# Another order of operand splits, gating steps and row tiles around the seven block products of a residual LoRA chain

## The reference

```python
x = x + x @ w_eff.T                      # layer 0: quantized weight plus a LoRA delta
x = x + (x @ W1.T + 2 * lora_1(x))       # layer 1: top-2 gates of 8 experts, rank 16 each
x = x + (x @ W2.T + b + 2 * lora_2(x))   # layer 2: one adapter per sequence, rank 16
x = x + x @ weight3[adapter].T           # layer 3: one full 1024x1024 matrix per sequence
```

## Time and profile before

| | |
|---|---|
| median of 3 runs | 658.16 us |
| the profiled execution: its time | 658.05 us |
| its span, first to last instruction | 656.2 us |
| TensorE busy | 644.5 us (98%) |
| VectorE busy | 499.8 us (76%) |
| ScalarE busy | 364.1 us (55%) |
| GpSimd busy | 89.0 us (14%) |
| DMA | 102 GB/s over the span |

### The profile page before, as it was taken

How to read it: one execution, slowest core, us unless ns; L and a number is a source line. 1 busy time by engine, 2 the same in 40 slices (tenths; PEclk the granted TensorE clock), 3 DMA queues, 4 the chain that set the end, 5 groups by cost and what they waited for, 6 DMA issues and landing times.

```text
span 656.2 us, 10322 instructions
## 1 busy us (share of the span) xinstructions
PE 644.5 (98%) x3992; PEld 591.0 (90%) x3992; DVE 499.8 (76%) x645; ACT 364.1 (55%) x549; POOL 89.0 (14%) x120
## 2 busy tenths in 40 slices
PE   8999999999999999899999999999999999999997
PEld 8899989999999999898889899889989889989886
DVE  6899899879970649858876967887886888686753
ACT  6673674961911445637664735664745665564553
POOL 2210225005010010001130001221001122000010
PEclk9999999999999999999999999999999999999999
DMA  9663112121021002132773122673213575002472
GB/s 295 190 200 91 33 35 62 33 62 35 1 64 64 1 1 89 33 97 72 231 237 98 52 75 61 197 255 124 65 33 97 162 258 182 1 1 65 127 229 94
DMA packets 46020, 67.32 MB, mean 103 GB/s; under 512 B 3604, under 2 KB 32020, under 8 KB 45972
## 3 DMA queue, kind: packets, MB, share of 16 engines
q1 hardware_dynamic: 40900, 58.28, 28.6%
q10 hardware_dynamic: 5072, 8.39, 3.5%
HBM read 58.27 MB, written 8.39 MB: 102 GB/s over the span
## 4 chain that ended last, share of the span: by engine, by line
PE 85%; DVE 13%; issue 1%; ACT 1%; DMA 1%; DVEq 0%; ACTq 0%
PE ps L1260 26%; PE ps L1262 26%; PE ps L1261 26%; DVE e_both L897 4%; PE ps L1403 3%; DVE x_both L897 2%; DVE tmp L1187 1%; PE ps L1271 1%; PE ps L1432 1%; PE ps L1405 1%; DMA xraw<-lora_b_t 1%; ACT e_both L683 1%; DVE bc_hi L897 1%; DVE e_mid_w L1160 0%; DVE e_mid_w L1123 0%
## 5 line engine op out<-in xcount | busy, mean ns | idle before, releaser
L1260 PE MATMUL ps<-e_both,ring_hi 128*128 128x384 f32 (+3 forms) x384 | 133.6, 348 | 0.0
L1262 PE MATMUL ps<-e_both,ring_lo 128*128 128x384 f32 (+3 forms) x384 | 133.5, 348 | 0.0
L1261 PE MATMUL ps<-x_both,e_both 128*128 128x256 f32 x448 | 125.6, 280 | 0.0
L897 DVE TENSOR_TENSOR e_both<-raw,e_both 128x512 fp32r<-128x512 f32 x128 | 90.3, 725 | 34.1 <-ACT e_both L771 33.4
L771 ACT ACTIVATE e_both<-raw 128x512 fp32r<-128x512 f32 x128 | 78.9, 628 | 67.0 <-PE ps L1262 66.7
L1260 PE MATMUL ps<-e_both,e_mid 128*128 128x512 f32 (+2 forms) x288 | 110.8, 385 | 0.0
L1262 PE MATMUL ps<-e_both,e_mid 128*128 128x512 f32 (+2 forms) x288 | 110.7, 384 | 0.0
L1261 PE MATMUL ps<-e_both,e_mid 128*128 128x512 f32 (+2 forms) x288 | 110.6, 384 | 0.0
L587 POOL TENSOR_TENSOR raw<-raw,ident 128x128 f32<-128x128 f32 x64 | 42.3, 662 | 360.7 <-DMA raw<-w_t 360.7
L1261 PEld LDWEIGHTS ps<-x_both,e_both 128*128 128x128 f32 x448 | 84.6, 189 | 0.0
L1262 PEld LDWEIGHTS ps<-e_both,ring_lo 128*128 128x128 f32 x384 | 72.3, 188 | 5.7
(11 more groups left out here) (175 smaller groups left out, 1271.0 us busy)
## 6 DMA issues: line engine op xcount, KB each, us to landing
raw<-w_t SPq DMA_DIRECT2D x64, 512.0 KB, 4.4
w_w<-x_t SPq DMA_DIRECT2D x16, 512.0 KB, 3.9
w_w<-w SPq DMA_DIRECT2D x15, 512.0 KB, 4.2
y<-tmp ACTq DMA_DIRECT2D x30, 256.0 KB, 3.5
e_both_w<-w_t SPq DMA_DIRECT2D x5, 512.0 KB, 7.7
e_both_w<-w_t SPq DMA_DIRECT2D x4, 384.0 KB, 6.0
e_mid_w<-bs SPq DMA_DIRECT2D x24, 64.0 KB, 2.9
e_mid_w<-b_cat SPq DMA_DIRECT2D x4, 128.0 KB, 5.9
```

What stands on the lines that cost most here:

```text
L897: return dve.tensor_tensor(out, whole, hi.bitcast(F32), ALU.subtract)
L1260: pe.matmul(out, a[0], b_[0], start=start, stop=False, **kw)
L1261: pe.matmul(out, a[0], b_[1], start=False, stop=False, **kw)
L1262: return pe.matmul(out, a[1], b_[0], start=False, stop=stop, **kw)
```

## The change

The change moves instructions within the four engines' streams of `group`, and swaps two loops. No instruction is added or removed.

- VectorE: the split of T3 moves from behind the gating to ahead of S2's split; S4's split moves from inside the gating to ahead of it; S3's split takes the place inside the gating; A12's follows the gating at once, ahead of the `bs` and T4 splits; `sum_block` on bank 0 moves ahead of `gt_lo`; A22's split moves ahead of the two additions to `h2_sum`.
- ScalarE: the `h2_tok` copies and the exponential move from around S4's split to behind the second `keep` of bank 0; A22's split moves ahead of `gt_hi` and the `h2_sum` copies.
- TensorE: `turn_h2` and `turn_g` move from between P3 and P4 to between P4 and P5; `h2_add` moves from between P4 and P5 to between P5 and P6. In `block_product` the row tiles m become the outer loop and the k tiles the inner one; the wait for the second half of the operand's low part comes after 6 matmuls rather than after 24.

```diff
 (ScalarE, group)
-                act.wait_ge(tok_done, g + 1)
-                act.wait_ge(h2_clear, 1)
-                for j in range(2):
-                    act.activation(h2_tok[:, 2 * j:2 * j + 2, R2 * j:R2 * (j + 1)],
-                                   tok[:, 2 * j:2 * j + 2, NOW_AT[j]:NOW_AT[j] + R2], ACT.Copy).then_inc(h2_tok_done, 1)
                 split_weight(g, "S4")
-                act.wait_ge(gate, GATE_STEPS * g + GATE_DV)
-                act.activation(gw[:, 1, :], gw[:, 0, :], ACT.Exp).then_inc(e_exp, 1)
                 act.wait_ge(prod, NP * g + 2)
                 keep(2, x3_sum[1][1], 4)
                 split_x(g, "T4")
                 split_weight(g, "S3")
                 act.wait_ge(prod, NP * g + 3)
                 keep(0, x3_sum[0][1], 0)
+                act.wait_ge(tok_done, g + 1)
+                act.wait_ge(h2_clear, 1)
+                for j in range(2):
+                    act.activation(h2_tok[:, 2 * j:2 * j + 2, R2 * j:R2 * (j + 1)],
+                                   tok[:, 2 * j:2 * j + 2, NOW_AT[j]:NOW_AT[j] + R2], ACT.Copy).then_inc(h2_tok_done, 1)
+                act.wait_ge(gate, GATE_STEPS * g + GATE_DV)
+                act.activation(gw[:, 1, :], gw[:, 0, :], ACT.Exp).then_inc(e_exp, 1)
                 split_weight(g, "A12")
+                split_weight(g, "A22")
                 act.wait_ge(gt_mm, g + 1)
                 act.activation(gt_hi, ps[:, 7, :], ACT.Copy).then_inc(gt_hi_done, 1)
...
-                split_weight(g, "A22")
 (VectorE, gating)
-                split_weight(g, "S4")
+                split_weight(g, "S3")
 (VectorE, group)
                 split_weight(g, "S1")
                 dve.tensor_tensor(s4_whole, weight[0][1], s2_whole, ALU.subtract).then_inc(e_add, 1)
+                split_x(g, "T3")
                 split_weight(g, "S2")
...
                 dve.tensor_tensor(s3_whole, weight[0][0], weight[1][0], ALU.subtract).then_inc(e_add, 1)
+                split_weight(g, "S4")
                 gating(g)
-                split_x(g, "T3")
+                split_weight(g, "A12")
...
                 split_x(g, "T4")
-                split_weight(g, "S3")
-                split_weight(g, "A12")
+                dve.wait_ge(prod, NP * g + 5)
+                dve.wait_ge(c_copy, 4 * g + 2)
+                sum_block(0, x3_sum[1][1], x3_sum[1][1])
                 dve.wait_ge(gt_hi_done, g + 1)
                 minus(gt_lo, ps[:, 7, :], gt_hi).then_inc(gt_done, 1)
+                split_weight(g, "A22")
                 dve.wait_ge(h2t_mm, g + 1)
...
-                dve.wait_ge(prod, NP * g + 5)
-                dve.wait_ge(c_copy, 4 * g + 2)
-                sum_block(0, x3_sum[1][1], x3_sum[1][1])
-                split_weight(g, "A22")
 (TensorE, block_product)
-                for k in range(4):
-                    if k % 2 == 0:
-                        pe.wait_ge(op_lo, 2 * NP * g + 2 * i + k // 2 + 1)
-                    for m in range(4):
+                for m in range(4):
+                    for k in range(4):
+                        if m == 0 and k % 2 == 0:
+                            pe.wait_ge(op_lo, 2 * NP * g + 2 * i + k // 2 + 1)
 (TensorE, group)
                 block_product(g, 3, False)
+                pe.wait_ge(c_copy, 4 * g + 3)
+                block_product(g, 4, False)
                 turn_h2(g)
                 turn_g(g)
-                pe.wait_ge(c_copy, 4 * g + 3)
-                block_product(g, 4, False)
+                block_product(g, 5, True)
                 h2_add(g)
-                block_product(g, 5, True)
                 pe.wait_ge(c_sum, 4 * g + 1)
                 block_product(g, 6, False)
```

## The result

The changed kernel takes 650.24 us (649.97 to 650.63, four runs) against 658.06 us: a ratio of 0.9881, interval 0.9864 to 0.9899. Forecast were 650.0 us and 649.3 to 653.0. The profiled execution took 650.05 us with a span of 648.3 us, 7.9 us less than before.

What follows compares the result with a forecast made beforehand. TensorE, busy for 644.5 of 656.2 us, bounds the kernel. Stalls of 4 x 1.72 + 0.62 + 3 x 0.21 = 8.13 us go: 658.05 - 8.13 = 649.9, median 0.1 higher, 650.0; range 649.3 to 653.

Steps and rivals of the forecast that it cites:

- The pool and the stalls: TensorE's 11.7 us of idle time as the most to win; late starts of P3 and P4, 8.13 us, to go.
- idle time of some 4 us: Sign that the forecast is right: TensorE's idle time falls from 11.7 us to some 4 us.
- The 0.10 us of the first matmul: A product's first matmul after a stall takes about 0.10 us longer; counted in the stalls at P3 and P4.
- The five transposes: On TensorE, between P4 and P5 in the new order: 0.55 us in group 1.
- The order of VectorE and ScalarE: Group 1 worked through: S3's split early by 1.5 us, A22's by 1.0, the last low-rank split covered by 2.0.
- The two margins of group 0: Group 0: S2's split early for P2 by 0.3 us, S3's for P4 by 0.95 us.
- Row tiles at no cost: Block products with row tiles outside, k inside, keep 118.2 ns per matmul: zero charged.
- The rival that the weight loads show: Row-tile order exposes weight loads in block products: 19.5 ns on 1344 matmuls, 26 us, giving 676 us; chance 0.05.
- The first rival: Splits stay a little late in the chain behind P4, 1.0 us per group: 654 us, case 651 to 655; chance 0.11.
- the cost to the gates' path: On ScalarE, A22 first in the strict queue order delays the gates' path by 2 us.
- The third rival: Something other than S3's split holds P4; only P3's stalls go, 1.25 us: 656.8 us; chance 0.04.
- a lost cover: Work no longer hidden behind TensorE costs its own length: `h2_add` without P6 3.6 us, S2's split some tenths.

Runs made afterwards that it cites:

- the old nest: The changed kernel with the block products' old loop nest, k tiles outside and row tiles inside: 650.10 us.
- the row tiles alone: The kernel before with only the two block-product loops swapped, row tiles outside: 661.46 us.
- A22 behind: The changed kernel with A22's high part on ScalarE back behind the copies of the turned gates and low-rank rows: 650.34 us.
- the S3 and T3 runs: The changed kernel with S3's split on VectorE behind the gating's second part: 664.53 us; separately, with T3's split back behind the gating: 662.13 us.
- the transposes late alone: The kernel before with only TensorE's transposes and h2 addition moved as in the change, old nest and old order on the other engines: 683.14 us.
- the transposes early: The changed kernel with transposes and h2 addition back at their old places on TensorE, new order on the other engines: 674.74 us.

## Why the prediction was right, point by point

- **The pool and the stalls.** 8.13 us of stalls were to go. Group 1 from P0 to `gates` shows what went; here are the two ends in the kernel before:
```profile
351.72 0.32 PE L1260 MATMUL ps<-x_pair,e_both 128*128 128x256 f32 x1
...
394.30 0.28 PE L1260 MATMUL ps<-bc_hi,br_hi 128*128 128x256 f32 x1
```
  That is 42.58 us, and 389.96 - 349.18 = 40.78 in the changed kernel: 1.80 us, where 1.93 was forecast. Group 0 gave 2.21 (forecast 2.34), all four 7.63. The other 0.3 us of the 7.9 lie ahead of P0 of group 0, in work that the change does not touch: P0 starts at 248.39 before and 248.07 after, and the other profiles put it between 247.96 and 248.55. That is scatter, and here it fell on the side that brings the two profiled executions nearer to the forecast.
- **A sign that did not come: idle time of some 4 us.** It is 5.4. The prediction took the 11.7 us of recorded idle time as all that can be won and its 8.13 us as a part of them. But it had sized the stalls from start to start. Recorded as idle were only P4's four waits, 5.8 us, and 0.37 at P3 of group 0, together 6.2, and by 6.3 the idle time fell; the rest lay in busy time, which fell from 644.5 to 642.9 us. The forecast did not hang on this: its 8.13 us come from the starts.
- **The terms that were off.** The 0.10 us of the first matmul was booked to the stall and taken as won; P5's first matmul, behind the transposes, still pays 0.08. P6, which has `gates` behind it, takes 5.75 us rather than 5.67, and P0 5.72; with the old nest they take 5.66 and 5.68. Why the nest costs P6 this much, the runs do not show (in the kernel before, the row tiles alone leave it at 5.66). The five transposes cost 0.46 us (377.54 to 378.00) and not 0.55, which goes the other way. Together some 0.1 us in each group, which is the whole miss.
- **The order of VectorE and ScalarE.** Worked through on the old trace's clock, with the new group 1 starting 2.55 us earlier: S4's split at 361.85 (measured 361.90), gating 364.15 (364.18), S3's split 368.05 (368.08), `gt_lo` 380.3 (380.26), A22's split 380.95 (380.87), the additions 384.5 (384.41). Margins 1.5, 1.0 and 2.0 us, measured 1.43, 0.99 and 2.05. No instruction changed its shape, and the durations from the old rows held; the new inputs were 0.26 us for each hand-over from TensorE and the estimate of 0.65 us for `gt_lo`, which took 0.69. The two margins of group 0 held as well: S2's split ends at 259.02 with P2 at 259.44 (0.4 us, forecast 0.3), S3's at 269.67 with P4 at 270.76 (1.1, forecast 0.95).
- **Row tiles at no cost.** Right within 0.1 us in each group, by the comparison of the nests. The rival that the weight loads show is out: 5.66 us for P1 to P4. P6's 5.75 us stand just at the bound that the prediction set for this rival, but 0.1 us in one product of seven is far from its 26 us. The prediction did not see that the nest alone, with late operands, costs time; in this change they are early.
- **The first rival**, splits a little late: not there, the chain behind P4 took the 5.7 us that were worked out (377.54 to 383.22). That `gt_hi` stands behind A22 costs VectorE 1.03 us of idle time and the end nothing. The prediction put the cost to the gates' path at 2 us; with A22 behind, `gt_lo` starts 7.27 us behind P4's start instead of 8.39, 1.1 us earlier, and the kernel takes the same time.
- **The third rival**, P4 held by something else: the S3 and T3 runs bring P4's wait back, each by itself, so both splits had to move, and behind the gating's second part is too late for S3.
- **What the prediction left out.** It priced a lost cover at its own length (`h2_add` 3.6 us, S2's split some tenths). The runs in which a cover was lost cost 1.3 to 2.3 us more in each group in which the clock fell. The time was right because no stall was left.

## What to carry to other kernels

When the bound engine waits at one place, lay out every engine's stream up to that place with the durations of the trace, each engine's instructions in the order in which they are written, and note for each hand-over by how much it is early: here that gave the start of every split compared above within 0.1 us. Moves on several engines that free one wait belong together, and any one of them left out can cost more than all of them bring. An inner loop that asks for a whole operand early is neutral while operands are early and costs when they are late, so settle the order of the producers first.

## What the runs showed of the hardware

A stall of TensorE can cost more than its length. In the kernel before, P4's wait of 1.46 us (four groups) left the granted clock at 1.00, and so did P4's wait of 2.0 us with the transposes late alone, in four groups of four. In the kernel with T3 late, 1.96 us of idle time were followed by a stretch at 0.50 in two groups of four; with S3 behind the gating, 2.0 us and a second gap for the second half, in three of four; with the row tiles alone, 1.46 us and a second gap of 0.10 us of recorded idle time six matmuls later, in two of four; with the transposes early, 3.7 us, and late alone, 4.0 us, in four of four. At the lower level a matmul of 256 columns took 0.213 us instead of 0.118, and P4 7.62 us instead of 6.09. Why it falls in one group and not in the next, with the same gaps, the runs do not show; the length of the gap alone does not settle it. The Trainium skill, "TensorE: Matmul & The Clock Gate", part 1, names two levels, 2.4 and 1.2 GHz. The granted clock of 1.00 and 0.50 agrees; the two spacings stand as 1.8 to 1, not quite as 2 to 1.
